# Softmax stage of a four-layer graph network: two rows' numerators on GpSimd, late rows' matmuls and copies placed earlier, products side by side

## The chip, the cores and the metric

One Trainium2 chip, of which the kernel uses one core. The metric is the device time of one execution in microseconds; three runs of the kernel before gave 9648.05 us as median (9647.0 to 9648.81). All numbers in the data are float32 at the kernel's border.

## What is computed

The reference runs four graph layers over 6250 nodes with 16 features and 206250 edges sorted by target node. The stage that the change touches is the second layer, an attention with one softmax for each of 256 channels (16 inputs times 16 outputs) over all edges that end in the same node:

```python
w_m = (efeat @ W_msg + b_msg).reshape(E, in_f, -1)
w_a = (efeat @ W_attn + b_attn).reshape(E, in_f, -1)
h_src = feat[src][:, :, None]
e1, e2 = w_m * h_src, w_a * h_src
seg_max = jax.ops.segment_max(e2, dst, num_segments=N)
ex = jnp.exp(e2 - seg_max[dst])
denom = jax.ops.segment_sum(ex, dst, num_segments=N)
ft = jax.ops.segment_sum(e1 * ex / denom[dst], dst, num_segments=N)
```

The other three layers (two convolutions, a relational layer, an edge network) gather and sum rows too, and are the same before and after.

## The kernel before

Each of 125 partitions holds 1650 successive edges. The softmax stage goes through them in 165 blocks of `B1` = 10 edges per partition, here called rows 0 to 9 of a block, each with 256 logits and 256 messages side by side (512 values). Three buffers, `s = b % 3`, hold successive blocks. One call of `soft(b, ...)` on each engine is one step. The engines run their own programs, written out by hand, and are tied only by counting semaphores.

In a step, for block b, whose predecessor is `o = b - 1`:

- **TensorE** multiplies edge features by weights into PSUM: rows 0 to 5 in three `products` of two rows, rows 6 to 9 (the late rows, `AT` = 6 onwards) one at a time in `scalable`, into two banks that are used in turn. It forms the differences between logits and running maxima with an identity and a negated identity (L1154 and L1155, six a step, the last a short one at L1158 and L1159), and two sums: `first_sum` (L1115, L1117) from the first row and the carried sum, `last_sum` (L1123, L1124) for the last row.
- **ScalarE** scales the late rows with the gathered features, 16 activations of 32 values a row (`scaled`, L809); takes six exponentials (L850, L853); and copies a first and a last row of sums (L817, L828).
- **VectorE** scales rows 0 to 5 (`product`, L1751, PSUM by gathered features), takes the running maxima forward and then backward (`top`, L1740 and L1744, 19 a step), and for block o forms the numerators (`weigh`, L1761: message times exponential), the carried sum (`carry`, L1770), and running sums along the rows (`row_sum`, L1783, rows 1 to 8). The order of these 35 instructions is written out in `soft`.
- **GpSimd** gathers 10 rows of node features a block with indirect DMAs (L595), four late ones first, which wait until ScalarE has finished with the block three before, and then six that wait for VectorE's products of that block. It works about four blocks ahead.
- **SyncE** loads features and flags and stores maxima and sums of each block.

`weigh(o, z, AT, NA)` covers the numerators of rows 6 to 9 in one instruction, between maxima 13 and 14. ScalarE's copy of the first late row of block b + 2 stands before exponential 4; TensorE's matmul for it stands before difference 4, and that for the second late row at the end of the step.

Of the kernel before, what the change touches and what calls it, by code (L numbers as in the profile page):

```python
# [14 lines left out]
P = 125  # L15
# [92 lines left out]
def graph_layers(nc, A, out):  # L108
# [5 lines left out]
    with ctx:  # L114
# [468 lines left out]
        def _(gp):  # L583
# [56 lines left out]
            gp.wait_ge(S("tab_conv2"), 16 * (NT + 1))  # L640
            narrow("conv2")

            gp.wait_ge(S("tab_feat"), 16 * (NT + 1))
            for b in range(NB1):
                s = b % 3
                if b >= 3:
                    gp.wait_ge(S("soft_ap"), NA * (b - 2))
                for t in range(AT, B1):
                    gather(GH[:, s, t, :], d_feat, srci[:, b * B1 + t:b * B1 + t + 1], f"soft_late_g{s}")
                for t in range(AT):  # L650
                    if b >= 3 and t % 2 == 0:
                        gp.wait_ge(S("soft_prod"), NG3 * (b - 3) + t // 2 + 1)
                    gather(GH[:, s, t, :], d_feat, srci[:, b * B1 + t:b * B1 + t + 1], f"soft_g{s}")
            for s in range(3):
                gp.wait_ge(S(f"soft_s{s}"), 160 * THIRD)
            for a, table in enumerate((d_smax, *d_sums)):
# [21 lines left out]
        def _(act):  # L678
# [117 lines left out]
            for c, (lo, hi) in enumerate(TAIL):  # L796
                root(f"ln2_{c}", lo, hi)

            def scaled(b, s, k, t):

                n = t - AT
                act.wait_ge(S("soft_am"), NA * b + n + 1)
                if n == 0:
                    act.wait_ge(S(f"soft_late_g{s}"), 16 * NA * (k + 1))
                    if not isinstance(b, int) or b >= 3:
                        act.wait_ge(S("soft_num"), 4 * (b - 2))
                bank = (4 + n % 2) * 512
                for i in range(F):
                    ins = act.activation(PB[:, s, n, 2 * F * i:2 * F * (i + 1)], PS[0:P, bank + 2 * F * i:bank + 2 * F * (i + 1)],  # L809
                                         ACT.Copy, scale=GH[:, s, t, i:i + 1])  # L810
                ins.then_inc(S("soft_ap"), 1)

            def first_rows(b, s):

# [15 lines left out]
            def soft(b, s, k, first, left):  # L830
                if left >= 1:
                    scaled(b + 1, (s + 1) % 3, k + (s == 2), AT + 1)
                if not first or s == 2:
                    last_rows(b - 2, (s + 1) % 3)
                if not first or s >= 1:
                    last_keep(b - 1, (s + 2) % 3)
                if left >= 1:
                    scaled(b + 1, (s + 1) % 3, k + (s == 2), AT + 2)
                if not first or s >= 1:
                    first_rows(b - 1, (s + 2) % 3)  # L840
                if left >= 1:
                    scaled(b + 1, (s + 1) % 3, k + (s == 2), AT + 3)
                for n in range(6):
                    if n == 4 and left >= 2:
                        scaled(b + 2, (s + 2) % 3, k + (s >= 1), AT)
                    act.wait_ge(S("soft_diff"), 6 * b + n + 1)
                    bank = PS[0:P, (6 + n % 2) * 512:(7 + n % 2) * 512]
                    if n < 5:
                        t = B1 - 2 - 2 * n
                        act.activation(paired(XD[:, s, t:t + 2, :], 0), bank.rearrange("p (x o) -> p x o", o=F), ACT.Exp)\  # L850
                           .then_inc(S("soft_exp"), 1)
                    else:
                        act.activation(DC, bank[:, 0:CH], ACT.Exp, bias=KR[:, s, 0, 0:1]).then_inc(S("soft_exp"), 1)  # L853

            act.wait_ge(S("h_soft"), 1)
            for t in range(AT, B1):
# [51 lines left out]
        def _(pe):  # L908
# [27 lines left out]
            pe.matmul(PS[0:R, 2560:2560 + F * F], small[0:NB, 480:480 + R], small[0:NB, 64:64 + F * F],  # L936
                      start=True, stop=True).then_inc(S("wrel_p"), 1)

            pe.wait_ge(S("diag"), 1)
            pe.matmul(PS[:, 3072:3072 + P], ones[0:P, :], diag[:, :], start=True, stop=True).then_inc(S("run_p"), 1)  # L940
            pe.wait_ge(S("setup"), 1)

# [167 lines left out]
            def first_sum(b, s):  # L1110

                pe.wait_ge(S("soft_exp"), 6 * b + 6)
                pe.wait_ge(S("soft_num"), 4 * b + 1)
                bank = PS[0:P, 3584:4096]
                pe.matmul(bank, ident[0:P, 0:P], XD[:, s, 0, :], start=True, stop=False)  # L1115
                pe.wait_ge(S("soft_carry"), b + 1)
                pe.matmul(bank, ident[0:P, 0:P], SC, start=False, stop=True).then_inc(S("soft_first"), 1)  # L1117
# [9 lines left out]
            def soft(b, s, k, first, left):  # L1127
# [7 lines left out]
                    products(b + 1, ahead, k1, 1)  # L1135

                for n in range(6):
                    if n == 4 and left >= 2:
                        scalable(b + 2, (s + 2) % 3, k + (s >= 1), AT)
                    if n == 4 and left >= 1:  # L1140
                        products(b + 1, ahead, k1, 2)
                    pe.wait_ge(S("soft_max"), MAXES * b + min(B1 + 1 + 2 * n, MAXES))
# [17 lines left out]
                if not first or s >= 1:  # L1160
                    pe.wait_ge(S("soft_exp"), 6 * b + 5)
                    last_sum(b - 1, (s + 2) % 3)
                if left >= 2:
                    scalable(b + 2, (s + 2) % 3, k + (s >= 1), AT + 1)

            products(0, 0, 0, 0)
            products(0, 0, 0, 1)
# [65 lines left out]
        def _(dve):  # L1233
# [116 lines left out]
            v.tensor_copy(small[0:NB, 480:480 + R], PS[0:NB, 2048:2048 + R]).then_inc(S("wa"), 1)  # L1350
            dve.wait_ge(S("wrel_p"), 1)
            v.tensor_copy(small[0:R, 640:640 + F * F], PS[0:R, 2560:2560 + F * F]).then_inc(S("wrel"), 1)
            v.tensor_scalar(diag[:, :], ident[0:P, 0:P], one_run[:, 0:1], None, ALU.mult).then_inc(S("diag"), 1)
            dve.wait_ge(S("run_p"), 1)
            link(v.tensor_copy(runT[:, :], PS[:, 3072:3072 + P]))
            v.tensor_scalar(resT[:, :], runT[:, :], 1.0, BIG, ALU.subtract, ALU.mult).then_inc(S("setup"), 1)
# [416 lines left out]
            def row_sum(b, s, t):  # L1773

                to, last = XD[:, s, t, :], XD[:, s, t - 1, :]
                if t == 1:
                    dve.wait_ge(S("soft_first"), b + 1)
                    last = PS[0:P, 3584:4096]
                else:
                    if t in (2, 4, 6):  # L1780
                        dve.wait_ge(S("soft_num"), 4 * b + t // 2 + 1)
                    dve.wait_ge(S("soft_sum"), (B1 - 2) * b + t - 1)
                v.scalar_tensor_tensor(to, last, KR[:, s, t, 1:2], to, ALU.mult, ALU.add).then_inc(S("soft_sum"), 1)  # L1783

# [6 lines left out]

            def late_sums(b, s):

                weigh(b, s, 0, 2)
                carry(b, s)
                row_sum(b, s, 1)
                weigh(b, s, 2, 2)
                row_sum(b, s, 2)
                row_sum(b, s, 3)
                weigh(b, s, 4, 2)  # L1800
                weigh(b, s, AT, NA)
                for t in range(4, B1 - 1):
                    row_sum(b, s, t)

# [12 lines left out]
            def soft(b, s, k, left):  # L1817
# [2 lines left out]
                dve.wait_ge(S(f"soft_k{s}"), 16 * (k + 1))  # L1820
                top(b, s, 0)
                product(b, s, 1)
                top(b, s, 1)
                top(b, s, 2)
                product(b, s, 2)
                top(b, s, 3)
                top(b, s, 4)
                weigh(o, z, 0, 2)
                top(b, s, 5)
                carry(o, z)  # L1830
                top(b, s, 6)
                top(b, s, 7)
                row_sum(o, z, 1)
                top(b, s, 8)
                weigh(o, z, 2, 2)
                top(b, s, 9)
                row_sum(o, z, 2)
                top(b, s, 10)
# [3 lines left out]
                top(b, s, 12)  # L1842
                row_sum(o, z, 4)
                top(b, s, 13)
                weigh(o, z, AT, NA)
                top(b, s, 14)
                row_sum(o, z, 5)
                top(b, s, 15)
                row_sum(o, z, 6)
                top(b, s, 16)  # L1850
                if left >= 1:
                    first_product(b + 1, (s + 1) % 3, k + (s == 2))
# [121 lines left out]
```

## Time and profile before

| | |
|---|---|
| median of three runs | 9648.05 us |
| the profiled execution | 9641.53 us |
| its span | 9639.7 us |
| mean granted TensorE clock | 0.92 of full |
| softmax stage in the span | about 2950 to 6350 us |
| busy over the span | PE 81%, DVE 76%, GpSimd (POOL) 70%, ACT 31% |

Times in the rows are microseconds from the start of the span. In a timeline a line is a start, a duration, the engine (PE is TensorE, DVE VectorE, ACT ScalarE, POOL GpSimd), the source line, the operation, its output and inputs with shape, how many successive instructions of the same kind are merged in it, and in brackets idle time of that engine in front of it with what released it. L12 is line 12 of the kernel.

### The profile page before, as it was taken

The page shows a single profiled execution, that of the slowest core. Times are in us where ns is not written, and L with a number is a line of the kernel's source. Part 1 is how long each engine was busy: PE and PEld are TensorE (multiplying, and loading weights), DVE is VectorE, ACT ScalarE, POOL GpSimd, SP SyncE. Part 2 cuts the span into 40 slices and gives each one's busy share as a digit, 9 for nine tenths or more (in the row PEclk, how much of TensorE's full clock was granted, in tenths as well). Part 3 has the DMA queues.
Part 4 walks back from the last instruction along what each step waited for, and adds up shares of the span by engine and source line. Part 5 has one row for each costly group of instructions (what it writes and reads, how often), then busy time and mean ns, then how long its engine had stood idle before and what let it go on. Part 6 is the DMA issues. An engine that isn't in the chain of part 4 may idle for free.

```text
span 9639.7 us, 129684 instructions
## 1 busy us (share of the span) xinstructions
PE 7836.6 (81%) x35619; PEld 4144.8 (43%) x35619; DVE 7327.0 (76%) x13039; ACT 3030.8 (31%) x12664; POOL 6745.5 (70%) x5111
## 2 busy tenths in 40 slices
PE   0799995999965888888888888845989896799994
PEld 0466663555532333333333333323556554455552
DVE  2566662555537999999999999987878875698884
ACT  0111111000005777777777777742000000000000
POOL 5577775788877766666666666635888887588887
PEclk6899996999988999999999999967999997899997
DMA  1344442233324777777777777766232321334332
GB/s 32 95 113 106 114 108 51 68 69 69 69 38 122 203 202 208 204 201 205 206 202 202 207 204 201 204 186 181 72 83 70 82 71 43 100 107 108 102 103 52
DMA packets 819396, 1219.98 MB, mean 127 GB/s; under 512 B 234445, under 2 KB 684119, under 8 KB 798513
## 3 DMA queue, kind: packets, MB, share of 16 engines
q1 hardware_dynamic: 574895, 1003.68, 34.8%
q0 software_dynamic: 208928, 107.90, 9.8%
q10 hardware_dynamic: 35440, 106.85, 3.5%
q8 instruction: 56, 0.92, 0.0%
q14 instruction: 77, 0.63, 0.0%
HBM read 423.03 MB, written 788.86 MB: 126 GB/s over the span
## 4 chain that ended last, share of the span: by engine, by line
POOL 35%; PE 28%; ACT 18%; issue 11%; DVE 5%; DMA 2%; SPq 1%; DVEq 0%; ACTq 0%; POOLq 0%
POOL arena L595 35%; ACT arena L809 15%; PE PS L986 10%; PE PS L1154 5%; PE PS L1155 4%; PE PS L1123 2%; PE PS L1010 2%; PE PS L1124 1%; ACT arena L850 1%; PE PS L969 1%; DVE arena L1916 1%; PE PS L1107 1%; PE PS L1115 1%; PE PS L989 1%; PE PS L1117 1%
## 5 line engine op out<-in xcount | busy, mean ns | idle before, releaser
L986 PE MATMUL PS<-arena,TB 128*128 128x500 bf16 x16038 | 3569.7, 377 | 184.7 <-DVE TB L1654 174.6
L595 POOL DMA_INDIRECT arena<-d_feat,srci x1650 | 2123.1, 1287 | 1241.2 <-ACT arena L809 757.4
L986 PEld LDWEIGHTS PS<-arena,TB 128*128 128x128 bf16 x16038 | 1567.0, 99 | 1851.1 <-issue 161.0
L595 POOL DMA_INDIRECT arena<-d_h,srci x1452 | 1870.0, 1288 | 610.4 <-issue 431.8
L809 ACT ACTIVATE arena<-PS,arena 125x32 f32<-125x32 f32 x10560 | 2012.1, 446 | 354.7 <-PE PS L1107 323.9
L1437 DVE TENSOR_SCALAR arena<-arena,lane 128x1500 bf16<-128x1500 f16 (+1 forms) x1848 | 1240.1, 728 | 575.4 <-DMA arena<-d_lane 340.1
L595 POOL DMA_INDIRECT arena<-d_rel,irel x858 | 1210.4, 1411 | 309.6 <-issue 261.2
L595 POOL DMA_INDIRECT arena<-d_nn,srci x726 | 1028.5, 1417 | 289.9 <-issue 220.7
L1154 PE MATMUL PS<-arena,ident 125*125 125x512 f32 x1650 | 959.0, 664 | 315.7 <-DVE arena L1744 210.1
L1449 DVE SCALAR_TENSOR_TENSOR arena<-arena,lane,PS 128x500 f32<-128x500 f16 x891 | 642.4, 722 | 737.1 <-PE PS L989 647.5
L1155 PE MATMUL PS<-arena 125*125 125x512 f32 x1650 | 883.9, 618 | 0.0
L1783 DVE SCALAR_TENSOR_TENSOR arena<-arena 125x512 f32<-125x512 f32 x1155 | 856.9, 742 | 0.3
L1740 DVE SCALAR_TENSOR_TENSOR arena<-arena 125x256 f32<-125x256 f32 x1650 | 786.5, 477 | 31.7
L1010 PEld LDWEIGHTS PS<-fold,arena 128*125 128x125 f32 x5280 | 696.6, 194 | 222.2 <-DVE arena L1449 94.0
L1010 PE MATMUL PS<-fold,arena 128*125 128x16 f32 (+1 forms) x5280 | 646.5, 255 | 121.4 <-ACT arena L719 108.4
L850 ACT ACTIVATE arena<-PS 125x512 f32<-125x512 f32 x825 | 566.0, 756 | 466.6 <-PE PS L1155 466.5
L1744 DVE SCALAR_TENSOR_TENSOR arena<-arena 125x256 f32<-125x256 f32 x1485 | 704.9, 475 | 0.4
L1469 DVE TENSOR_TENSOR_SCAN arena<-keep,arena 125x50 f32<-125x50 f32 x2640 | 585.5, 295 | 107.4 <-DMA arena<-d_h,srci 98.6
L1751 DVE TENSOR_TENSOR arena<-PS,arena 125x1024 f32<-125x1024 f32 x495 | 600.9, 1214 | 38.6 <-DMA arena<-d_feat,srci 33.4
L1154 PEld LDWEIGHTS PS<-arena,ident 125*125 125x125 f32 x1650 | 270.3, 196 | 796.0 <-issue 462.9
L704 ACT ACTIVATE arena<-PS 125x448 f32<-125x448 f32 x66 | 35.9, 543 | 1663.1 <-PE PS L1010 1663.1
L1761 DVE TENSOR_TENSOR arena<-arena 125x512 f32<-125x512 f32 (+1 forms) x660 | 545.1, 826 | 3.5 <-ACT arena L850 3.5
(285 smaller groups left out, 7679.0 us busy)
## 6 DMA issues: line engine op xcount, KB each, us to landing
d_smax<-arena SPq DMA_DIRECT2D x165, 1120.0 KB
d_sums_low<-arena SPq DMA_DIRECT2D x330, 560.0 KB
d_sums_high<-arena SPq DMA_DIRECT2D x330, 560.0 KB
arena<-d_pick SPq DMA_DIRECT2D x99, 875.0 KB
arena<-d_lane SPq DMA_DIRECT2D x99, 546.9 KB
d_x<-arena ACTq DMA_DIRECT2D x165, 241.7 KB
arena<-d_x SPq DMA_DIRECT2D x165, 241.7 KB
d_rel<-arena SPq DMA_DIRECT2D x50, 669.4 KB
```

Of the source, the lines that this page charges most:

```text
L595: gp.indirect_dma_start(out=dst, out_offset=None, in_=table, in_offset=bass.IndirectOffsetOnAxis(ap=index, axis=0)).then_inc(S(sem), 16)
L809: ins = act.activation(PB[:, s, n, 2 * F * i:2 * F * (i + 1)], PS[0:P, bank + 2 * F * i:bank + 2 * F * (i + 1)], ACT.Copy, scale=GH[:, s, ...
L850: act.activation(paired(XD[:, s, t:t + 2, :], 0), bank.rearrange("p (x o) -> p x o", o=F), ACT.Exp)\
L986: pe.matmul(PS[:, acc_at(L, q):acc_at(L, q) + w], TB[:, part, g * LANES * F:(g + 1) * LANES * F], OH[L][i][:, g, at:at + w], start=g == 0 ...
L1010: ins = pe.matmul(PS[0:P, 3584 + t * w:3584 + (t + 1) * w], lanes, fold[:, 0:w], start=True, stop=True)
L1154: pe.matmul(bank.rearrange("p (x o) -> p x o", o=F), ident[0:P, 0:P], paired(pairs, 0), start=True, stop=False)
L1155: pe.matmul(bank, neg, XM[:, s, t:t + 2, :].rearrange("p t c -> p (t c)"), start=False, stop=True)\
L1437: ins = v.tensor_scalar(OH[L][i][:, c, 0:n], PI[L][s][:, at:at + n], lane[:, c:c + 1], None, ALU.is_equal)
L1449: v.scalar_tensor_tensor(MK[L][:, acc_slot(L, q), 0:n], LI[L][s][:, q * QW:q * QW + n], lane[:, NG:NG + 1], PS[:, acc_at(L, q):acc_at(L, q ...
L1740: v.scalar_tensor_tensor(wide_row(XM[:, s, n, :]), wide_row(prev), KR[:, s, n, 0:1], logits, ALU.add, ALU.max).then_inc(S("soft_max"), 1)
L1744: v.scalar_tensor_tensor(XM[:, s, t, :], XM[:, s, t + 1, :], KR[:, s, t + 1, 0:1], XM[:, s, t, :], ALU.add, ALU.max).then_inc(S("soft_max" ...
L1783: v.scalar_tensor_tensor(to, last, KR[:, s, t, 1:2], to, ALU.mult, ALU.add).then_inc(S("soft_sum"), 1)
```

## The change

GpSimd takes over the numerators of the last two rows of each block, as an instruction of its own program between the third and the fourth late gather, once the first exponential of that block and maximum 0 of the next block are there. VectorE's `weigh` for rows 6 to 9 shrinks to rows 6 and 7 and comes early in the step; product 2 follows product 1 directly; the other sums and numerators move accordingly. TensorE's matmuls for the first two late rows of block b + 2 stand before differences 1 and 2. ScalarE's 16 copies of the first late row are issued 5, 5 and 6 at a time, behind exponentials 1, 2 and 3. A semaphore of the set-up is merged with another.

```diff
+            def last_numerators(b):
+                s = b % 3
+                gp.wait_ge(S("soft_exp"), 6 * b + 1)
+                if b < NB1 - 1:
+                    gp.wait_ge(S("soft_max"), MAXES * (b + 1) + 1)
+                rows = XD[:, s, B1 - 2:B1, :]
+                gp.tensor_tensor(paired(rows, 1), paired(PB[:, s, NA - 2:NA], 1), paired(rows, 0), ALU.mult)\
+                    .then_inc(S("soft_gp_num"), 1)
...
                 for t in range(AT, B1):
                     gather(GH[:, s, t, :], d_feat, ..., f"soft_late_g{s}")
+                    if b >= 4 and t == B1 - 2:
+                        last_numerators(b - 4)
...
+            for b in range(NB1 - 4, NB1):
+                last_numerators(b)
...
-            def scaled(b, s, k, t):
+            def scaled(b, s, k, t, lo=0, hi=F):
...
-                        act.wait_ge(S("soft_num"), 4 * (b - 2))
+                        act.wait_ge(S("soft_num"), 4 * (b - 3) + 1)
+                        act.wait_ge(S("soft_gp_num"), b - 2)
...
                 for n in range(6):
-                    if n == 4 and left >= 2:
-                        scaled(b + 2, (s + 2) % 3, k + (s >= 1), AT)
                     act.wait_ge(S("soft_diff"), 6 * b + n + 1)
...
+                    if 1 <= n <= 3 and left >= 2:
+                        scaled(b + 2, (s + 2) % 3, k + (s >= 1), AT, 5 * n - 5, 5 * n if n < 3 else F)
...
-                pe.wait_ge(S("soft_num"), 4 * b + 1)
+                pe.wait_ge(S("soft_num"), 4 * b + 2)
...
-                    if n == 4 and left >= 2:
-                        scalable(b + 2, (s + 2) % 3, k + (s >= 1), AT)
+                    if n in (1, 2) and left >= 2:
+                        scalable(b + 2, (s + 2) % 3, k + (s >= 1), AT + n - 1)
...
-                if left >= 2:
-                    scalable(b + 2, (s + 2) % 3, k + (s >= 1), AT + 1)
...
-                    if t in (2, 4, 6):
-                        dve.wait_ge(S("soft_num"), 4 * b + t // 2 + 1)
+                    if t in (2, 4):
+                        dve.wait_ge(S("soft_num"), 4 * b + t // 2 + 2)
+                    if t == B1 - 2:
+                        dve.wait_ge(S("soft_gp_num"), b + 1)
```

VectorE's order in a step after the change, in short (top n is maximum n): top 0, product 1, product 2, top 1, weigh rows 6 and 7, top 2, top 3, weigh rows 0 and 1, top 4, carry, top 5, weigh rows 2 and 3, top 6, top 7, row sum 1, top 8, top 9, row sum 2, top 10, row sum 3, top 11, weigh rows 4 and 5, top 12, row sum 4, top 13, row sum 5, top 14, row sum 6, top 15, top 16, product 0 of the next block, top 17, row sum 7, top 18, row sum 8.

Before it was: top 0, product 1, top 1, top 2, product 2, top 3, top 4, weigh rows 0 and 1, top 5, carry, top 6, top 7, row sum 1, top 8, weigh rows 2 and 3, top 9, row sum 2, top 10, row sum 3, top 11, weigh rows 4 and 5, top 12, row sum 4, top 13, weigh rows 6 to 9, top 14, row sum 5, top 15, row sum 6, top 16, product 0 of the next block, top 17, row sum 7, top 18, row sum 8.

## Rows read from the trace of the kernel before

**Rows 1.** The page: busy time by engine; VectorE's busy tenths in 40 slices.
```profile
PE 7836.6 (81%) x35619; PEld 4144.8 (43%) x35619; DVE 7327.0 (76%) x13039; ACT 3030.8 (31%) x12664; POOL 6745.5 (70%) x5111
...
DVE  2566662555537999999999999987878875698884
```

**Rows 2.** Windows of 200 us: length, busy PE, PEld, DVE, ACT, POOL, clock, DMA.
```profile
3200.00:3400.00 200.00, 164.26 (x409) 64.60 (x409) 195.96 (x343) 154.24 (x716) 147.18 (x104) 1.00 0.74 205
...
3600.00:3800.00 200.00, 171.72 (x412) 71.61 (x412) 195.89 (x342) 152.64 (x704) 124.26 (x100) 0.93 0.73 202
```

**Rows 3.** Timeline of VectorE: row sum 8 of block 0, then one step.
```profile
3008.48 0.74 DVE L1783 SCALAR_TENSOR_TENSOR arena<-arena 125x512 f32<-125x512 f32 x1
...
3029.66 0.47 DVE L1740 SCALAR_TENSOR_TENSOR arena<-arena 125x256 f32<-125x256 f32 x1
3030.06 1.21 DVE L1751 TENSOR_TENSOR arena<-PS,arena 125x1024 f32<-125x1024 f32 x1
3031.19 0.98 DVE L1740 SCALAR_TENSOR_TENSOR arena<-arena 125x256 f32<-125x256 f32 x2
...
3033.23 0.99 DVE L1740 SCALAR_TENSOR_TENSOR arena<-arena 125x256 f32<-125x256 f32 x2
3034.14 0.68 DVE L1761 TENSOR_TENSOR arena<-arena 125x512 f32<-125x512 f32 x1
...
3035.14 0.68 DVE L1770 TENSOR_TENSOR arena<-PS,arena 125x512 f32<-125x512 f32 x1
3035.74 1.08 DVE L1740 SCALAR_TENSOR_TENSOR arena<-arena 125x256 f32<-125x256 f32 x2
3037.03 0.75 DVE L1783 SCALAR_TENSOR_TENSOR arena<-PS,arena 125x512 f32<-125x512 f32 x1 [0.22 <-PE PS L1117]
...
3043.27 1.22 DVE L1761 TENSOR_TENSOR arena<-arena 125x1024 f32<-125x1024 f32 x1
3044.41 0.47 DVE L1744 SCALAR_TENSOR_TENSOR arena<-arena 125x256 f32<-125x256 f32 x1
...
3050.17 0.47 DVE L1740 SCALAR_TENSOR_TENSOR arena<-arena 125x256 f32<-125x256 f32 x1
```

**Rows 4.** Timeline of TensorE in a step with a low clock.
```profile
4520.42 1.64 PE L1154 MATMUL PS<-arena,ident 125*125 125x512 f32 x2 [1.11 <-DVE arena L1744]
...
4529.74 1.03 PE L1154 MATMUL PS<-arena,ident 125*125 125x512 f32 x2
...
4533.35 1.12 PE L1123 MATMUL PS<-arena 125*125 125x512 f32 x2 [0.85 <-ACT arena L850]
4534.31 1.02 PE L1124 MATMUL PS<-arena,ident 125*125 125x512 f32 x2
```

**Rows 5.** Timeline of ScalarE in the same step.
```profile
4529.79 2.95 ACT L809 ACTIVATE arena<-PS,arena 125x32 f32<-125x32 f32 x16
4532.50 0.72 ACT L850 ACTIVATE arena<-PS 125x512 f32<-125x512 f32 x1
```

**Rows 6.** Timeline of GpSimd: gathers early in the stage, then the settled state.
```profile
3017.21 1.21 POOL L595 DMA_INDIRECT arena<-d_feat,srci  x1 [0.31 <-issue]
...
3031.52 1.22 POOL L595 DMA_INDIRECT arena<-d_feat,srci  x1 [0.30 <-issue]
...
3041.23 1.75 POOL L595 DMA_INDIRECT arena<-d_feat,srci  x1 [0.30 <-issue]
...
3043.28 2.29 POOL L595 DMA_INDIRECT arena<-d_feat,srci  x1 [0.30 <-issue]
...
3048.39 1.22 POOL L595 DMA_INDIRECT arena<-d_feat,srci  x1 [0.31 <-DVE arena L1751]
...
4504.43 1.56 POOL L595 DMA_INDIRECT arena<-d_feat,srci  x1 [5.20 <-ACT arena L809]
...
4518.58 1.23 POOL L595 DMA_INDIRECT arena<-d_feat,srci  x1 [0.30 <-issue]
```

**Rows 7.** Groups of instructions on GpSimd that compute: busy time, mean ns of one.
```profile
L589 POOL TENSOR_SCALAR_AFFINE_SELECT ident<-ident 128x128 f32<-128x128 f32 x1 | 0.3, 292 | 0.2 <-POOL ident L587 0.2
```

## What the change does to the time

> **What bounds the kernel now.** I read the page first: over the whole span TensorE is busy 81% and VectorE 76%, but VectorE's row of slices stands at 9 from slice 13 to 26, and at 5 to 8 on most of the rest [rows 1]. That stretch, about 2980 to 6350 us, is the softmax stage, 165 blocks, and the change touches nothing else of weight. Two windows inside it show VectorE busy 196 of 200 us whatever clock TensorE is granted, 1.00 in one and 0.93 in the other, with the DMA share at 0.74 and 0.73 [rows 2]. So I went to VectorE's timeline and took one step apart, from the first max of a block to the first max of the next: 3029.66 to 3050.17, which is 20.51 us [rows 3]. There are 35 instructions in it and one recorded idle, 0.22 us before the first row sum of the block (3037.03), released by TensorE's L1117. 164 calls of `soft` at 20.51 us are 3364 us.
>
> What counts is the distance from one start to the next, not the duration, because VectorE's instructions overlap by about 0.08 us. By starts, the numerators of four rows (L1761, 1024 elements) cost 3044.41 - 3043.27 = 1.14 us; a 512-element operation of the same kind (L1770) costs 3035.74 - 3035.14 = 0.60; a product 3031.19 - 3030.06 = 1.13; a pair of directly dependent maxima 3034.14 - 3033.23 = 0.91, where two with other work between them take 3030.06 - 3029.66 = 0.40 each. A direct dependence therefore costs 0.91 - 0.80 = 0.11 [rows 3].
>
> TensorE and ScalarE form a second loop that is nearly as long. Where the clock is low, the first difference of a step starts at 4520.42 (its pair of passes at L1154 takes 1.64 us, against 1.03 at 4529.74), difference 4 at 4529.74, and the last sum L1123 at 4533.35, held by exponential 4 at 4532.50, which itself stood behind 16 copies at L809 that began at 4529.79 [rows 4, 5]. GpSimd is the third resource: in the settled state its ten gathers run from 4504.43 to 4518.58 + 1.23, and it sits idle 5.20 us before them, waiting for ScalarE's copies [rows 6].
>
> **The change, part by part.**
> (1) VectorE's numerators of rows 6 to 9 become numerators of rows 6 and 7: 1.14 becomes 0.60, so -0.54 us a step.
> (2) The order on VectorE. Before, the maxima pairs (1,2), (3,4) and (6,7) are adjacent; after it (2,3), (6,7), (8,9) and (15,16): +0.11. The slot of maxima 6 and 7 up to the first row sum is now 3037.03 - 3035.74 = 1.29 us, since the row sum waits for TensorE's sum behind the carry. A plain pair is 0.91, so 0.38 us of it is waiting. After the change, numerators (0.60) stand between the carry and those maxima, which is more than the 0.38 needed, so -0.38. Sum for VectorE: -0.54 + 0.11 - 0.38 = -0.81, a step of 19.70 us.
> (3) Product 2 moved up behind product 1: its matmuls are issued before difference 4 of the step before, and that starts at 4529.74, while product 2 would start more than 1.5 us later. Nothing waits.
> (4) ScalarE's copies of a late row, in parts behind exponentials 1, 2 and 3. Exponentials come one difference apart, about 1.7 us (twice the distance from 4533.35 to 4534.31 at least), and an exponential plus five copies (five sixteenths of 2.7 us) need about 1.4; they fit. Exponential 4 no longer stands behind 16 copies. It can start 1.06 us after the second half of difference 4, at about 4531.67 instead of 4532.50, and TensorE carries one matmul of 0.22 more ahead of it (row AT+1, which stood at the end of the step before). TensorE's loop in the low clock: first difference to last sum 4533.35 - 4520.42 = 12.93, less 0.83, plus 0.22, so about 12.3; last sum 4535.33 - 4533.35 = 1.98 [rows 4]; then on VectorE carry to maximum 10, in the new order 0.60 + 0.40 + 0.60 + 0.91 + 0.67 + 0.91 + 0.67 + 0.48, plus 0.23 to TensorE, 5.5. Together 19.8, practically VectorE's 19.70. If ScalarE's parts didn't fit, the 0.83 would come back; in the full clock there is over a microsecond of room. I take +0.05 a step for it, with 0 and +0.4 as bounds.
> (5) GpSimd's operation, 512 elements, two inputs. The trace of before has no such operation. Nearest rows: AFFINE_SELECT on 128 elements takes 0.292 us [rows 7], so four times that is 1.17, and VectorE's own 0.60 by starts; an instruction twice as slow per element as AFFINE_SELECT would be 2.3. I take 1.2, with 0.6 and 2.3 as ends, because AFFINE_SELECT is the only computation of any size on this engine here. It waits for maximum 0 of the next block, so it runs from about +0.6 to +1.8 us of a step; the two products cover VectorE from +0.40 to +2.66. What is queued behind it on GpSimd: one late gather and six early ones, then the wait for the copies and three more. In the early part of the stage, where GpSimd has not caught up, the trace shows how this queue runs: seven gathers from 3031.52 (+1.86) to 3041.23 + 1.75 (+13.32), and three more from 3043.28 (+13.62) to 3048.39 + 1.22 (+19.95) [rows 6]. The operation would be ready for +19.70 + 0.6 = +20.3. So the 5.20 us of idle are nearly all spent: the gathers themselves grow, 2.29 us at 3043.28 against 1.22 at 3031.52, according to what VectorE runs at that moment. GpSimd fits into 19.7 us with a few tenths to spare. I take +0.10 for slips, bounds 0 and +0.5.
> By the Trainium skill's "GPSIMD Engine Reference", section 3.1, a two-input operation costs about 2.6 cycles an element at 1.2 GHz; an estimate from that page is 1.1 us for 512 elements, and the sum would be the same.
> (6) The start. Numerators of block 0 on GpSimd stand behind 43 gathers. The 43rd starts at 3017.21 and ends at 3018.42; with the operation about 3019.6 [rows 6]. Row sum 8 of block 0, which now waits for it, ran at 3008.48 [rows 3]. That is a stall of about 10 us, once; its bounds are 5 and 16.
> (7) Renamed semaphore in the set-up, and four numerators behind the last gathers: nothing; both beside waits that are there.
>
> **Sum.** 164 x (-0.81 + 0.05 + 0.10) = -108, plus 10, so -98 us. The profiled execution took 9641.5 us (span 9639.7), the median 9648.05; 9641.5 - 98 = 9543.5, plus the 6.5 us by which the median stands above it: 9550.
>
> **Rivals.**
> *A, GpSimd becomes the bound.* Before it has caught up, GpSimd does nine gathers from 3031.52 to 3048.39, 1.87 us each [rows 6]; ten are 18.7, with the operation at 1.2 and an issue gap of 0.3 that is 20.2, and with an operation of 1.5 us 20.5. For it: the idle is spent, and VectorE now waits for its result in row sum 8. Against: the settled order lets GpSimd gather beside the products. At 20.25 us a step: -0.26 x 164 + 10 = -33, 9615 us.
> *B, VectorE is held up by GpSimd's operation (slower).* The trace shows one direction only: a gather stretches from 1.22 to 2.29 us by what VectorE runs. If a GpSimd operation of 1.2 us in turn holds VectorE, and it doesn't fall beside the products, a step is 19.70 + 1.2 = 20.9, +0.39 x 164 + 10 = +74, 9722 us. It decides from 0.81 us held per step. The start puts GpSimd out of place by up to 18 us, so some steps will see this; but there a VectorE at 20.9 is slower than GpSimd at 20.2, so GpSimd gains 0.7 us a step and should be back beside products (any of the three) within some twenty-five steps. An operation of 2.3 us or more would reach this case from the other side: 18.7 + 2.3 + 0.3 = 21.3 on GpSimd itself.
> The Trainium skill, "SBUF — State Buffer", section "SBUF: two separate sides", states that VectorE and GpSimd share one pair of ports as an exclusive lock held for a whole instruction, for a VectorE operation with two SBUF inputs against a GpSimd operation that reads SBUF. A product has one input in PSUM, so by that rule beside the products nothing is held and elsewhere all of it is: it gives forecast or rival B by place. The lengthened gathers agree with the rule; no row here shows VectorE held.
> *C, nothing moves.* The loop over ScalarE and TensorE is longer than I made it (part 4 at +0.4, GpSimd at +0.4): 164 x -0.01 + 10, 9656 us. Against: in the full clock window VectorE is as busy as in the low one [rows 2], so that loop doesn't set the step.
>
> **Chances.** Forecast 0.64 (steps of 19.6 to 20.1 us, 9490 to 9585); A 0.14; C 0.07; B 0.15. Range: the forecast's best is -0.95 x 164 = -156, 9492; above, it takes in A and C and the mild end of B, 9670; what lies beyond is most of B. 0.2% of this kernel is 19 us, about what a measurement can tell from no change. Faster: forecast and most of A, 0.76; within 0.2%: C and a little of A, 0.08; slower: 0.16.
>
> **What would show it.** VectorE's numerators of two rows at 0.60 by starts, no idle before row sum 1, a step of 19.7 to 19.9; the last sum L1123 no longer behind an exponential that stands behind 16 copies; GpSimd's operation of about 1.2 us starting 0.1 to 0.2 us after maximum 0, with VectorE's product and maximum 1 undelayed; GpSimd idle before its late gathers down from 5.20 us to under one; one stall near 10 us at row sum 8 of block 0. Wrong if GpSimd's operation is over 2 us, if VectorE shows gaps while it runs, or if GpSimd never catches up and row sum 8 waits in every step.

## The result

The changed kernel takes 9566.03 us (median; 9564.78 to 9567.54), the kernel before 9647.52 in the same comparison, ratio 0.9912 with a 95% interval of 0.9901 to 0.9924. That is 81.5 us less; 9550 was forecast, 98 less. The profiled execution has a span of 9565.3 us.

The page of the changed kernel, busy time by engine and VectorE's busy tenths, against [rows 1]:

```profile
PE 7830.7 (82%) x35619; PEld 4232.1 (44%) x35619; DVE 7251.5 (76%) x13039; ACT 3104.1 (32%) x12664; POOL 7388.2 (77%) x5276
...
DVE  2566662555535999999999999986887885698884
```

VectorE does as many instructions in 75 us less. GpSimd is busy 643 us longer with only 165 more instructions: 215 us of that are the new ones, and 382 us the gathers of this stage (2504.9 against 2123.1 us). Two windows of 200 us, against [rows 2], columns as there:

```profile
3200.00:3400.00 200.00, 170.91 (x421) 74.07 (x421) 196.82 (x353) 162.97 (x734) 165.80 (x111) 0.94 0.78 211
3600.00:3800.00 200.00, 170.52 (x420) 73.35 (x419) 195.67 (x350) 161.97 (x730) 166.74 (x111) 0.94 0.77 209
```

VectorE is as full as before and gets through 353 instructions instead of 343. It is still the bound. Its timeline over one step of the changed kernel, against [rows 3]:

```profile
4505.31 0.48 DVE L1755 SCALAR_TENSOR_TENSOR arena<-arena 125x256 f32<-125x256 f32 x1
4505.70 2.35 DVE L1766 TENSOR_TENSOR arena<-PS,arena 125x1024 f32<-125x1024 f32 x2
4507.97 0.47 DVE L1755 SCALAR_TENSOR_TENSOR arena<-arena 125x256 f32<-125x256 f32 x1
4508.36 0.68 DVE L1776 TENSOR_TENSOR arena<-arena 125x512 f32<-125x512 f32 x1
4508.96 1.00 DVE L1755 SCALAR_TENSOR_TENSOR arena<-arena 125x256 f32<-125x256 f32 x2
4509.88 0.68 DVE L1776 TENSOR_TENSOR arena<-arena 125x512 f32<-125x512 f32 x1
4510.48 0.48 DVE L1755 SCALAR_TENSOR_TENSOR arena<-arena 125x256 f32<-125x256 f32 x1
4510.91 0.69 DVE L1785 TENSOR_TENSOR arena<-PS,arena 125x512 f32<-125x512 f32 x1
...
4512.51 1.09 DVE L1755 SCALAR_TENSOR_TENSOR arena<-arena 125x256 f32<-125x256 f32 x2
4513.52 0.75 DVE L1800 SCALAR_TENSOR_TENSOR arena<-PS,arena 125x512 f32<-125x512 f32 x1
4514.18 1.08 DVE L1755 SCALAR_TENSOR_TENSOR arena<-arena 125x256 f32<-125x256 f32 x2
4515.18 0.75 DVE L1800 SCALAR_TENSOR_TENSOR arena<-arena 125x512 f32<-125x512 f32 x1
...
4525.24 0.48 DVE L1755 SCALAR_TENSOR_TENSOR arena<-arena 125x256 f32<-125x256 f32 x1
```

The step is 4525.24 - 4505.31 = 19.93 us; over 150 steps it is 19.92 on average, against 20.56 before, and the commonest length is 19.89. The numerators of rows 6 and 7 cost 4508.96 - 4508.36 = 0.60. The idle before the first row sum is gone (4513.52). What was not foreseen are the pairs of maxima (6,7) and (8,9): 4513.52 - 4512.51 = 1.01 and 4515.18 - 4514.18 = 1.00, where the pair (2,3) costs 4509.88 - 4508.96 = 0.92.

GpSimd in the same step, against [rows 6]:

```profile
4499.71 2.99 POOL L595 DMA_INDIRECT arena<-d_feat,srci  x1 [0.58 <-ACT arena L825]
4503.00 1.21 POOL L595 DMA_INDIRECT arena<-d_feat,srci  x1 [0.30 <-issue]
4504.52 1.29 POOL L595 DMA_INDIRECT arena<-d_feat,srci  x1 [0.30 <-issue]
4505.94 1.29 POOL L650 TENSOR_TENSOR arena<-arena 125x512 f32<-125x512 f32 x1
4507.41 1.24 POOL L595 DMA_INDIRECT arena<-d_feat,srci  x1 [0.19 <-issue]
```

The operation takes 1.29 us, from 4505.94 to 4507.23, wholly within VectorE's two products (4505.70 to 4507.97), and maximum 0 ends at 4505.79. The idle of 5.20 us before the late gathers is 0.58. The first late gather takes 2.99 us. It begins in VectorE's stretch without products and ends at 4502.70, 0.64 us after the start of the product at 4502.06.

TensorE's loop in this step, which has a low clock: the first difference began at 4496.63, and the last sum, against [rows 4]:

```profile
4508.82 1.12 PE L1140 MATMUL PS<-arena 125*125 125x512 f32 x2
4509.78 1.02 PE L1141 MATMUL PS<-arena,ident 125*125 125x512 f32 x2
```

From that first difference to the last sum are 12.19 us, with no wait for an exponential in front of the sum (0.85 before), and its end at 4510.80 is just ahead of the carry at 4510.91, which comes 0.04 later than its turn. So in a step whose first matmuls have a low clock (0.64 of full granted from 4497 to 4501) the two loops are level. In the next step, with the full clock throughout, the first difference is at 4516.56 and the last sum at 4527.53, which is 10.97 us: there TensorE has over a microsecond of room.

The start of the stage: the first row sum 8, and then the operations of two blocks, which fall outside the products (VectorE, then GpSimd):

```profile
3019.56 0.75 DVE L1800 SCALAR_TENSOR_TENSOR arena<-arena 125x512 f32<-125x512 f32 x1 [11.53 <-POOL arena L650]
...
3035.94 2.66 DVE L1800 SCALAR_TENSOR_TENSOR arena<-arena 125x512 f32<-125x512 f32 x1
...
3053.62 2.63 DVE L1755 SCALAR_TENSOR_TENSOR arena<-arena 125x256 f32<-125x256 f32 x2
3056.18 0.74 DVE L1800 SCALAR_TENSOR_TENSOR arena<-arena 125x512 f32<-125x512 f32 x1
```
```profile
3036.74 1.30 POOL L650 TENSOR_TENSOR arena<-arena 125x512 f32<-125x512 f32 x1
...
3054.66 1.29 POOL L650 TENSOR_TENSOR arena<-arena 125x512 f32<-125x512 f32 x1
```

Row sum 8 of block 0 comes 3019.56 - 3008.48 = 11.1 us later than before [rows 3]. The steps from the next maximum 0 (3020.23) on are 24.56, 21.43, 21.62 and 21.94 us long, and 19.94 from the fifth on; the four cost 9.9 us more than four settled ones. In each of them one piece of VectorE's work is held by GpSimd's operation, that is, it ends only after the operation has ended: the row sum at 3035.94 (2.66 us instead of 0.75), the pair of maxima at 3053.62 (2.56 us by starts instead of 1.00), and one maximum in each of the other two (2.15 and 1.77 instead of 0.48). Together that is 6.4 us. The other 3.4 us are waits behind the stall: in the first step 0.81 for ScalarE and 1.95 for TensorE's last sum, in the fourth 0.63 for a product's matmul. The start of a record doesn't tell who goes first: the row sum's begins 0.80 us before the operation's, and it is held all the same.

It isn't the kind of instruction that decides. In the changed kernel run again (the last experiment) it is a numerator TENSOR_TENSOR with both inputs in SBUF that is held, 2.53 us instead of 0.68, while each product with an input in PSUM beside which an operation runs, over 300 in either run, takes 1.21 or 1.22 us:

```profile
3070.10 2.53 DVE L1776 TENSOR_TENSOR arena<-arena 125x512 f32<-125x512 f32 x1
```
```profile
3070.78 1.29 POOL L650 TENSOR_TENSOR arena<-arena 125x512 f32<-125x512 f32 x1
```

### The profile page after: what moved, and what is told of

Read it like the earlier page. It is cut to its first block, busy times and chain, and to the rows that moved or that the text cites. A ratio compares the mean times of both kernels' runs of the same rounds, so it can differ in the third digit from the quotient of the medians.

```text
span 9565.3 us, 130175 instructions
## 1 busy us (share of the span) xinstructions
PE 7830.7 (82%) x35619; PEld 4232.1 (44%) x35619; DVE 7251.5 (76%) x13039; ACT 3104.1 (32%) x12664; POOL 7388.2 (77%) x5276
## 4 chain that ended last, share of the span: by engine, by line
POOL 36%; issue 25%; DVE 19%; PE 15%; DMA 2%; DVEq 1%; SPq 1%; ACT 0%; POOLq 0%; ACTq 0%
POOL arena L595 36%; PE PS L1003 10%; DVE arena L1755 6%; DVE arena L1759 4%; DVE arena L1800 3%; PE PS L1027 2%; DVE arena L1776 1%; DVE arena L1766 1%; PE PS L986 1%; DVEq L1747 1%; DVE arena L1933 1%; PE PS L1006 1%; DMA arena<-d_lane 1%; DVE arena L1464 0%; PE PS L1171 0%
## 5 line engine op out<-in xcount | busy, mean ns | idle before, releaser
L595 POOL DMA_INDIRECT arena<-d_feat,srci x1650 | 2504.9, 1518 | 554.5 <-issue 434.7
L595 POOL DMA_INDIRECT arena<-d_h,srci x1452 | 1910.3, 1316 | 570.8 <-issue 440.2
L1172 PE MATMUL PS<-arena 125*125 125x512 f32 x1650 | 929.1, 647 | 0.0
L865 ACT ACTIVATE arena<-PS 125x512 f32<-125x512 f32 x825 | 512.6, 621 | 516.7 <-PE PS L1172 516.7
L1171 PEld LDWEIGHTS PS<-arena,ident 125*125 125x125 f32 x1650 | 314.3, 204 | 772.1 <-issue 647.5
L1172 PEld LDWEIGHTS PS<-arena 125*125 125x125 f32 x1650 | 339.9, 206 | 463.3 <-issue 463.3
```

Of the source, the lines that this page charges most:

```text
L595: gp.indirect_dma_start(out=dst, out_offset=None, in_=table, in_offset=bass.IndirectOffsetOnAxis(ap=index, axis=0)).then_inc(S(sem), 16)
L1171: pe.matmul(bank.rearrange("p (x o) -> p x o", o=F), ident[0:P, 0:P], paired(pairs, 0), start=True, stop=False)
L1172: pe.matmul(bank, neg, XM[:, s, t:t + 2, :].rearrange("p t c -> p (t c)"), start=False, stop=True)\
```

## The experiments

**GpSimd's operation taken out, the rest kept.**

```diff
-                    if b >= 4 and t == B1 - 2:
-                        last_numerators(b - 4)
...
-                weigh(o, z, AT, NA - 2)
+                weigh(o, z, AT, NA)
```

The four calls behind the last gathers and the waits of ScalarE and VectorE for the operation go too.

> The changed kernel with GpSimd's operation taken out again: VectorE weighs rows 6 to 9 in one instruction (1.14 us by starts) at the new early place; order, matmuls and split copies stay as changed. Theory (VectorE's instructions by starts set the step): the step is 19.91 + 0.54 = 20.45 us, the stall at row sum 8 of block 0 (11.5 us) and the long first steps (9.9 us together) are gone: 9566 + 0.54 x 162 - 21 = 9632 us. Rival (the order of VectorE's instructions and the freed exponential bring most of it, GpSimd little): under 9600. Rival (GpSimd's operation brings all of it): 9648 or more.

Measured: 9629.1 us, ratio to before 0.9981 (0.9971 to 0.9990). The common step is 20.42, with one of 21.25 about every fifteenth (0.8 us of waiting for a matmul in front of a product), 20.47 on average; there is no stall and there are no long steps at the start. Order, matmuls and split copies alone are worth 18 us; GpSimd's part, with the others there, 63.

**GpSimd's operation alone, the rest as in the kernel before.**

```diff
+                    if b >= 4 and t == B1 - 2:
+                        last_numerators(b - 4)
...
                 top(b, s, 13)
-                weigh(o, z, AT, NA)
+                weigh(o, z, AT, NA - 2)
                 top(b, s, 14)
```

> The kernel before with the numerators of rows 8 and 9 on GpSimd as its only change: VectorE's order, the copies and the late matmuls stay as they were, numerators of rows 6 and 7 (0.60 us by starts) at the old place behind maximum 13. By VectorE's sum alone the step would be 20.51 - 0.54 = 19.97, plus about 0.2 for the operation that outlasts product 1: 20.2. Theory (two loops, each at about 20.5 us before): the loop over TensorE and ScalarE, 12.93 + 1.98 + about 5.4, holds it at 20.4 or more, and with the start's 21 us the time is 9640 to 9670, no gain at all. Rival (the parts add up, and the order and copies alone were worth 18 us): 9566 + 18 = 9584 us.

Measured: 9685.7 us, ratio 1.0037 (1.0023 to 1.0051), so slower than before. The profiled execution was the fastest of five (9650.5 us), the other four took 9683 to 9689: the trace shows why nothing is gained, and not where those 35 us went. The parts don't add up, as expected; the reason is another one. TensorE's loop doesn't hold VectorE here: the only wait in nearly every step is the old 0.22 before row sum 1. The short steps are 20.17 us, in which maximum 1 is held by 0.2, as expected. In 56 of 150 steps the operation starts late, and most of these are 21.15 us long (GpSimd, then VectorE, in one of them):

```profile
3531.60 2.35 POOL L595 DMA_INDIRECT arena<-d_feat,srci  x1 [2.22 <-ACT arena L824]
3534.25 1.23 POOL L595 DMA_INDIRECT arena<-d_feat,srci  x1 [0.30 <-issue]
3535.78 1.80 POOL L595 DMA_INDIRECT arena<-d_feat,srci  x1 [0.31 <-issue]
3537.61 1.30 POOL L650 TENSOR_TENSOR arena<-arena 125x512 f32<-125x512 f32 x1
```
```profile
3536.43 1.20 DVE L1766 TENSOR_TENSOR arena<-PS,arena 125x1024 f32<-125x1024 f32 x1
3537.57 2.15 DVE L1755 SCALAR_TENSOR_TENSOR arena<-arena 125x256 f32<-125x256 f32 x2
3539.64 1.22 DVE L1766 TENSOR_TENSOR arena<-PS,arena 125x1024 f32<-125x1024 f32 x1
```

GpSimd waits 2.22 us for ScalarE's late copies, its three gathers then end past maximum 0, and the operation starts at 3537.61, when product 1 is over. It holds the two maxima: 3539.64 - 3537.57 = 2.07 us instead of 0.91. The average is 20.54.

**Product 2 moved away from product 1.**

```diff
                 product(b, s, 1)
-                product(b, s, 2)
                 top(b, s, 1)
                 weigh(o, z, AT, NA - 2)
+                product(b, s, 2)
```

> The changed kernel with product 2 moved back by two instructions (behind maximum 1 and the numerators of rows 6 and 7), so that GpSimd's operation, which runs from +0.6 to +1.9 us of a step, meets maximum 1 and the numerators from +1.5 on. Theory (GpSimd's operation holds VectorE's instructions with two SBUF inputs and not the products): maximum 1 waits until about +1.95, a step of 19.91 + 0.4 = 20.3 us, 9630 us. Rival (no holding; only the start of the stage showed it for another reason): 9566 us within 5.

Measured: 9644.8 us, ratio 1.0000 (0.9990 to 1.0010): one product moved by two places takes the whole gain away. Maximum 1 is held in every step, by 0.2 us (GpSimd's operation, then VectorE, with a row from the next step):

```profile
3982.64 1.28 POOL L650 TENSOR_TENSOR arena<-arena 125x512 f32<-125x512 f32 x1
```
```profile
3983.54 0.67 DVE L1755 SCALAR_TENSOR_TENSOR arena<-arena 125x256 f32<-125x256 f32 x1
...
4009.02 0.69 DVE L1785 TENSOR_TENSOR arena<-PS,arena 125x512 f32<-125x512 f32 x1 [1.04 <-PE PS L1141]
```

That makes steps of 20.11, half of the expected 0.4. The rest is the wait in the last row: in every third step the carry waits 1.04 us for TensorE's last sum. In the step shown the first difference is at 3993.44, the granted clock was 0.59 of full from 3992 to 3996 and 0.55 from 3996 to 4000, and from that difference to the last sum it is 13.5 us, not 12.2. Why the clock is lower in these steps than in the changed kernel's was not looked into. So the holding is shown, and it accounts for 29 us of 150 steps; another 47 us are waits for TensorE.

**GpSimd's operation in the stretch without products.**

```diff
-                    gp.wait_ge(S("soft_max"), MAXES * (b + 1) + 1)
+                    gp.wait_ge(S("soft_max"), MAXES * (b + 1) + 10)
```

> The changed kernel with GpSimd's operation released by maximum 9 of the next block instead of maximum 0, so that it falls into the stretch without products. Theory (held for the whole operation, as the two places at the start showed, 1.56 and 1.67 us): the step is 19.91 + 1.5 to 1.7 = 21.4 to 21.6 us, 9566 + 1.6 x 160 = 9820 us, slower than the kernel before. Rival (GpSimd is held and VectorE is not): the step stays 19.9, 9566 to 9580 us.

Measured: 9764.7 us, ratio 1.0121 (1.0104 to 1.0137). GpSimd, then VectorE:

```profile
4007.14 1.65 POOL L650 TENSOR_TENSOR arena<-arena 125x512 f32<-125x512 f32 x1 [3.43 <-DVE arena L1755]
```
```profile
4006.90 0.75 DVE L1800 SCALAR_TENSOR_TENSOR arena<-arena 125x512 f32<-125x512 f32 x1
4007.56 1.51 DVE L1759 SCALAR_TENSOR_TENSOR arena<-arena 125x256 f32<-125x256 f32 x1
4008.99 0.74 DVE L1800 SCALAR_TENSOR_TENSOR arena<-arena 125x512 f32<-125x512 f32 x1
```

The operation itself grows from 1.29 to 1.65 us, since a row sum of VectorE is under way at 4007.14, and then holds the next maximum: 1.43 us by starts instead of 0.40. So 1.03 us are lost, not 1.6: here the row sum that VectorE has begun is finished first, unlike the one at 3035.94 in the changed kernel. The two cases differ in what GpSimd did before, a wait of 3.43 us here and a gather there; whether that decides was not tried. The common step is 20.97, and two in nine are 22.2 or 22.3: in these VectorE also waits 0.6 to 0.8 us for a product's matmul and 0.4 for TensorE's last sum. This is rival B as a kernel: slower than before.

**The late matmuls and copies back in their old places.**

```diff
                 for n in range(6):
+                    if n == 4 and left >= 2:
+                        scaled(b + 2, (s + 2) % 3, k + (s >= 1), AT)
                     act.wait_ge(S("soft_diff"), 6 * b + n + 1)
...
-                    if 1 <= n <= 3 and left >= 2:
-                        scaled(b + 2, (s + 2) % 3, k + (s >= 1), AT, 5 * n - 5, 5 * n if n < 3 else F)
...
-                    if n in (1, 2) and left >= 2:
-                        scalable(b + 2, (s + 2) % 3, k + (s >= 1), AT + n - 1)
+                    if n == 4 and left >= 2:
+                        scalable(b + 2, (s + 2) % 3, k + (s >= 1), AT)
...
+                if left >= 2:
+                    scalable(b + 2, (s + 2) % 3, k + (s >= 1), AT + 1)
```

> The changed kernel with only the late rows' matmuls and ScalarE's 16 copies put back to their old places (before difference 4, before exponential 4, end of the step). Theory of the prediction (part 4): TensorE's and ScalarE's loop becomes 12.93 + 1.98 + 5.5 = 20.4 us in the low clock, so the step goes from 19.91 to 20.2 to 20.4 and the time to 9615 to 9645 us. Rival: VectorE's sum alone sets the step and the copies are hidden anyway: 9566 us within 5.

Measured: 9652.7 us (9644 to 9666), ratio 1.0005 (0.9995 to 1.0015); 87 us lost, more than expected. Steps wander between 19.89 and 22.7 with 20.53 on average. VectorE's waits from 3200 to 6200 us (engine, line, what it waited for, us in total, times, longest):

```profile
DVE arena L1787 <- PE PS L1141: 47.8, 104, 1.1
DVE arena L1768 <- DMA d_sums_high<-arena: 23.5, 50, 1.0
```

The first is the loop over TensorE, as forecast. The second was not: the product that uses a buffer again waits for the store of what was in it. In the changed kernel this wait doesn't appear. By the program ScalarE copies the last rows, which the store waits for, behind the second late row's copies, and with these late the store would be late too; that chain is argued from the code and wasn't tried by itself. GpSimd's operation plays no part: in 150 steps it starts 0.62 to 0.64 us after maximum 0, as in the changed kernel, and no instruction of VectorE is held.

**The copies in one piece behind exponential 3.**

```diff
-                    if 1 <= n <= 3 and left >= 2:
-                        scaled(b + 2, (s + 2) % 3, k + (s >= 1), AT, 5 * n - 5, 5 * n if n < 3 else F)
+                    if n == 3 and left >= 2:
+                        scaled(b + 2, (s + 2) % 3, k + (s >= 1), AT)
```

> The changed kernel with ScalarE's 16 copies of the first late row in one piece behind exponential 3 instead of in parts behind exponentials 1, 2 and 3; late matmuls stay early. Exponential 4 comes 2.15 us after the start of exponential 3 when TensorE is ready; 0.49 + 2.7 us of work now stand between them, so it is 1.0 us late. Theory (TensorE's loop has next to no room in its low clock): the step grows by 0.3 to 1.0 us, 9610 to 9700 us. Rival (only the place of the matmuls counts): 9566 within 5.

Measured: 9737.4 us, ratio 1.0088 (1.0071 to 1.0104), beyond the expected span. The common wait, TensorE and VectorE:

```profile
4005.56 1.12 PE L1140 MATMUL PS<-arena 125*125 125x512 f32 x2 [1.09 <-ACT arena L865]
```
```profile
4007.64 0.69 DVE L1785 TENSOR_TENSOR arena<-PS,arena 125x512 f32<-125x512 f32 x1 [1.10 <-PE PS L1141]
```

Exponential 4 is late by a microsecond, the last sum with it, and the carry with that: the whole of it arrives at VectorE, without anything taken up on the way. The steps are 21.06 on average. About one in six lasts 22.4 us; in these VectorE also waits some 0.8 us for a product's matmul and 0.4 for an exponential. One in five is 19.88 without any wait. What makes the steps differ is left open.

**One wait for the four late rows.**

```diff
-                if AT <= n < B1:
-                    dve.wait_ge(S("soft_ap"), NA * b + n - AT + 1)
+                if n == AT:
+                    dve.wait_ge(S("soft_ap"), NA * (b + 1))
```

> The changed kernel, but VectorE waits for ScalarE's four scaled late rows of a block once, at maximum 6, instead of at each of the maxima 6, 7, 8 and 9. In the changed kernel the dependent pairs (6,7) and (8,9) take 1.00 us by starts inside the hardware loop and 0.92 in the last steps, which stand outside it; the pairs without this second wait take 0.92 everywhere. Theory (the second wait costs 0.09 us in a dependent pair): both pairs 0.92, the step 19.91 - 0.18 = 19.73 us, 9566 - 28 = 9538 us. Rival (the 0.09 belongs to reading the late rows, or to what ScalarE does meanwhile): the pairs stay at 1.00 and the time at 9566 within 5.

Measured: 9535.1 us, ratio 0.9887 (0.9871 to 0.9902); the changed kernel beside it on the same chip 9562.0. The two pairs now take 4502.10 - 4501.18 = 0.92 and 4503.67 - 4502.76 = 0.91:

```profile
4501.18 1.00 DVE L1755 SCALAR_TENSOR_TENSOR arena<-arena 125x256 f32<-125x256 f32 x2
4502.10 0.74 DVE L1800 SCALAR_TENSOR_TENSOR arena<-PS,arena 125x512 f32<-125x512 f32 x1
4502.76 1.00 DVE L1755 SCALAR_TENSOR_TENSOR arena<-arena 125x256 f32<-125x256 f32 x2
4503.67 0.75 DVE L1800 SCALAR_TENSOR_TENSOR arena<-arena 125x512 f32<-125x512 f32 x1
```

The common step is 19.72 us. The gain is 27 us of 28 expected, so the waits in front of maxima 7, 8 and 9 cost that time, though no idle is recorded for them. But it isn't so that any second wait costs something. The pair of maxima (3,4) of the kernel before has one too, since maximum 4 waits for a product, and takes 3034.14 - 3033.23 = 0.91 [rows 3]. The trace shows a difference: in front of the second maximum of (6,7) and (8,9) in the loop it records a register operation of VectorE's sequencer (ALU_OP), with 0.59 to 0.60 us from the first start to the second; in front of maximum 4 before it records a plain semaphore instruction (EVENT_SEMAPHORE), with 0.51; and with one wait nothing, with 0.51. In the last steps, which are written out behind the loop, it records nothing between the two either, so they don't show a second wait that is free. That the register operation costs the 0.09 us fits all of these rows, but the pair (3,4) also differs in that it waits for VectorE's own products and not for ScalarE; the two were not tried apart.

**The operation 13 gathers earlier in GpSimd's program.**

```diff
                 if b >= 3:
+                    last_numerators(b - 3)
                     gp.wait_ge(S("soft_ap"), NA * (b - 2))
...
-                    if b >= 4 and t == B1 - 2:
-                        last_numerators(b - 4)
...
-            for b in range(NB1 - 4, NB1):
+            for b in range(NB1 - 3, NB1):
```

> The changed kernel, but GpSimd takes the numerators of block c before its late gathers of block c + 3, 13 gathers earlier in its program. Theory (the stall of 11.5 us and the four long first steps, 9.9 us more, come from the operation's place behind 43 gathers): both nearly gone, the step the same 19.91, 9566 - 15 to 21 = 9545 to 9551 us. Rival (GpSimd now waits for maximum 0 with less of a lead and is late for the gathers): steps longer than 19.95, 9566 or more.

Measured: 9541.4 us, ratio 0.9896 (0.9881 to 0.9911), 20.7 us less than the changed kernel beside it. Step 3 begins at 3035.73 instead of 3044.79, and it and the two steps after it are 19.89 us at once. The next one is 21.25, with waits of 0.77 and 0.40 us for TensorE; then the steps are settled, with 19.91 on average over 150, as in the changed kernel.

**Both, and the changed kernel again.**

> Both edits together: one wait for the late rows and the operation 13 gathers earlier. If both theories hold: 9566 - 28 - 18 = 9520 us. If GpSimd is the next bound (its idle in the changed kernel is 0.58 us a step), the step stays over 19.80 us and the time over 9530 us.

> The changed kernel itself on the chip of the two edits, as their reference: 9566 us within 5.

Measured: 9518.1 us with both edits, ratio 0.9867 (0.9852 to 0.9882), and 9562.0 for the changed kernel, 0.9917 (0.9903 to 0.9930). The two edits together save 43.9 us, of 47.6 that they save one by one, and the step is 19.75 on average, as with the first edit alone: GpSimd is not the next bound at this point. This kernel is faster than the changed kernel and than either edit by itself.

## Why the prediction was right

*Numerators, part 1.* 1.14 became 0.60 by starts, as said. Shown twice: by the rows and by the run without the operation, which gives the 0.5 us a step back.

*Order on VectorE, part 2.* This term was mis-sized by 0.19, in two places. I took 0.91 for a dependent pair of maxima from pair (3,4), but the pairs of late rows take 1.00 inside the loop. So of the 1.29 us between maximum 6 and the first row sum not 0.38 but 0.28 was waiting, and only that went (1.01 now); and the pair (8,9) that the new order makes costs 0.20 and not 0.11. With the measured terms, 20.51 - 0.54 - 0.28 + 0.20 = 19.89, which is the commonest step; the sum was 19.70, and the kernel with one wait has 19.72. I had the row for it [rows 3]: the pair at 3035.74 lasts 1.08 us and the one at 3033.23 0.99, and I read the difference as part of the waiting.

*Slips of TensorE's and GpSimd's loops, 0.05 and 0.10.* They cover by luck most of what part 2 lacked, so that the step was forecast 0.66 shorter and is 0.64 shorter. TensorE's was measured at about 0.04 in the steps with a low clock (12.19 us against 12.3 forecast, the carry just behind it). GpSimd's is zero in the settled state. The lower end of the range, 0.95 us a step, is more than the 0.81 that the terms give without any slip, so it had nothing behind it; the result is far from it.

*Products side by side, part 3,* and *the operation, part 5.* 1.29 us against 1.2, released by maximum 0, beside the products, VectorE undelayed; idle before the late gathers 0.58, "under one". I had said that GpSimd fits with a few tenths to spare. It has none to see, since a gather ends at 4505.81 and maximum 0 at 4505.79, but its gathers have slack in them: one takes 2.99 us where others take 1.21, which I put down to waiting for VectorE.

*Copies, part 4.* The 1.7 us between exponentials stood beside rows that make 1.92; measured are 1.71 to 1.94, so the parts of the copies fit either way. The part is right in what it does, too small in what it costs when missing: I gave up to 0.4 us a step, and the runs show 0.6 (copies back) and 1.1 (in one piece). Besides TensorE's loop two things can hang on it that I had not named: a wait for a store appeared when the copies were late, and GpSimd's gathers are released by the late copies. The second made the operation late only in the run with GpSimd's operation alone; with the copies back in the changed kernel it was on time.

*The start, part 6.* The stall: 11.1 us for 10. But the one omission that cost most is here: rival B said that GpSimd is out of place at the start "so some steps will see this", and the sum had nothing for it. Four long steps cost 9.9 us, 6.4 of them held by GpSimd and the rest waits behind the stall. With the measured terms, 162 x (20.56 - 19.92) = 104, less 11 and 10, gives 83, and 81.5 were measured. Of the 16.5 us between the forecast and that, 10 are the long steps, 4 the steps themselves (108 against 104) and 1 the stall. The agreement within 2 us is no finer evidence than that: from the start of the stage's last step to the end, which the change hardly touches, the profiled execution before took 3300.0 us, the changed kernel's 3308.2 and its second one 3302.2.

*The rivals.* A did not come: from the fifth of the steps above on, the length is VectorE's own. B is real as a mechanism. The direction that no row of before could show, GpSimd holding VectorE, costs 0.2 us where the operation outlasts a product a little and 1.0 to 1.9 where it falls elsewhere; the kernel escapes it by the place of the operation alone. The Trainium skill's rule of the shared, exclusively held pair of ports ("SBUF — State Buffer", "SBUF: two separate sides") agrees with the runs in both respects: beside products, with one input in PSUM, nothing is held (1.21 to 1.22 us each), and elsewhere it is (2.53 us instead of 0.68). C did not come.

## What to carry to other kernels

When an engine is full, an operation moved to an idle neighbour is worth its distance between starts, but only where it meets nothing of the first engine's that it holds: place it beside instructions that it leaves alone, and check that its own engine gets there in time, also in the first steps. Where two loops are level, taking work out of one gives little until the other is shortened too (with the copies back in their old places nothing was left of the gain), and one part alone can cost time, as GpSimd's did here when its operation came late. Look at the waits between directly dependent instructions of a full engine: one that is always met long before can still cost (here 0.09 us each, in a loop, where the trace has a register operation in front of it), and one wait for the last of several events can stand for them all.

## What the runs showed of the hardware

- A GpSimd TENSOR_TENSOR on 512 float32 values a partition takes 1.29 us; the next gather follows after 0.19 us, where gathers are 0.30 apart.
- Such an operation delays VectorE's instructions that read two operands from SBUF until it has ended (1.03 us in the settled state of one run, 1.16 for a pair in another, up to 1.91 at the start). It was itself delayed by one that had begun in one run (1.65 instead of 1.29), and at the start it held one whose record began 0.80 us earlier. Products, with an input in PSUM, were never delayed by it.
- A gather issued by GpSimd takes 1.21 to 1.25 us when it starts while a product runs (300 in 150 steps of the changed kernel). The others take 1.21 to 3.06, and those over 1.8 all end while a product runs.
- A second wait in front of a directly dependent VectorE instruction costs 0.09 us inside the hardware loop where the trace records a register operation for it, and nothing where it records a plain semaphore instruction (0.91 us for the pair (3,4) before). That the register operation is the cause was not tried by itself.
